# Spectra of a correlation attention by pairs of float32r products, accumulated on fixed PSUM banks

## What is computed

```python
x = x + autocorrelation(layernorm(x), ctx, ctx)        # B, L, D = 8, 512, 2048
x = x + ffn(layernorm(x))                              # w 2048x2048, bias, LoRA adapters of rank 32

corr = ifft(fft(q, axis=L) * conj(fft(k, axis=L))).real    # along L, per column
w, idx = top_k(corr, 12); w = softmax(w)
out[pos] = sum_i w_i * v[min(idx_i + pos, L - 1)]          # the index is clamped at the last row
```

## Time and profile before

| what | value |
|---|---|
| runs | 3445.2, 3446.3, 3446.85 us; median 3446.3 |
| profiled execution | 3438.6 us, its span 3436.8 us, clock 0.983 |
| PE busy | 3280.5 us (95%) |
| DVE, POOL, ACT busy | 2006.3, 1574.0, 931.3 us |
| steps 2 to 16 (from the transposes of n=1 to those of n=16) | 788.56 us, 52.57 us each |
| steps 18 to 31 (from n=17 to n=31) | 740.34 us, 52.88 us each |
| the step between them | 70.72 us |
| last step and way into the last block | 76.03 us |
| last block | 1541.7 us |

### The profile page before, as it was taken

One profiled execution on the slowest core, in us unless ns is written; L12 is line 12 of the kernel. 1 busy time (PEld: TensorE's weight loads), 2 busy tenths in 40 slices (PEclk: granted clock), 3 DMA queues, 4 the chain that ended last, 5 costly groups with the idle time before them and its releaser, 6 DMA issues. The chain is left out here.

```text
span 3436.8 us, 38078 instructions
## 1 busy us (share of the span) xinstructions
PE 3280.5 (95%) x14592; PEld 1639.7 (48%) x14592; DVE 2006.3 (58%) x2768; ACT 931.3 (27%) x1559; POOL 1574.0 (46%) x727
## 2 busy tenths in 40 slices
PE   7699999999999999999995999999999999999999
PEld 4354554554544455455542444444444444444444
DVE  4289989999888999998985232232323232232321
ACT  1434444344334444544432110111101110111100
POOL 0587888878868888887862110111001110111000
PEclk9799999999999999999998999999999999999999
DMA  7133243342342334234223611011110111011110
GB/s 310 70 113 132 98 153 110 119 153 100 129 152 108 140 127 177 103 126 147 84 101 124 228 50 59 37 38 59 50 54 29 59 49 59 37 38 59 50 50 25
DMA packets 125328, 335.59 MB, mean 98 GB/s; under 512 B 7648, under 2 KB 24160, under 8 KB 108800
## 3 DMA queue, kind: packets, MB, share of 16 engines
q1 hardware_dynamic: 125184, 333.64, 27.1%
HBM read 245.27 MB, written 88.34 MB: 97 GB/s over the span
## 5 line engine op out<-in xcount | busy, mean ns | idle before, releaser
L1248 PE MATMUL ps<-w_hi,h_hi 128*128 128x512 f16 x2048 | 780.0, 381 | 18.4 <-issue 16.9
L1250 PE MATMUL ps<-w_hi,h_lo 128*128 128x512 f16 x2048 | 779.1, 380 | 0.0
L1249 PE MATMUL ps<-w_lo,h_hi 128*128 128x512 f16 x2048 | 778.9, 380 | 0.0
L1143 POOL TENSOR_TENSOR rp<-ve,half 128x1 f32<-128x1 f32 x32 | 17.6, 549 | 1243.7 <-DVE ve L1301 1243.7
L1355 DVE SCALAR_TENSOR_TENSOR xt<-ps,w_back,xt 128x512 f32<-128x512 f32 x128 | 96.0, 750 | 757.1 <-PE ps L1250 756.1
L826 PE MATMUL ps<-op,it 128*128 128x512 f32 x1024 | 448.1, 596 | 21.0 <-DVE op L956 21.0
L752 PE MATMUL ps<-wt,fp 128*128 128x512 f16 x1536 | 339.1, 381 | 9.9 <-ACT spo L639 6.9
L1248 PEld LDWEIGHTS ps<-w_hi,h_hi 128*128 128x128 f16 x2048 | 200.9, 98 | 258.0 <-issue 27.2
L826 PEld LDWEIGHTS ps<-op,it 128*128 128x128 f32 x1024 | 195.7, 191 | 267.8 <-issue 262.3
L1250 PEld LDWEIGHTS ps<-w_hi,h_lo 128*128 128x128 f16 x2048 | 201.0, 98 | 243.9 <-issue 3.9
L1249 PEld LDWEIGHTS ps<-w_lo,h_hi 128*128 128x128 f16 x2048 | 201.0, 98 | 228.9 <-issue 3.3
(11 more groups left out here) (149 smaller groups left out, 5235.3 us busy)
## 6 DMA issues: line engine op xcount, KB each, us to landing
cg<-ctx SPq DMA_DIRECT2D x32, 1024.0 KB, 7.1
xg<-x SPq DMA_DIRECT2D x32, 1024.0 KB, 9.5
xv<-x SPq DMA_DIRECT2D x32, 1024.0 KB
x_scratch<-xv SPq DMA_DIRECT2D x32, 1024.0 KB, 7.4
xt<-x_scratch SPq DMA_DIRECT2D x32, 1024.0 KB, 5.0
out<-xt SPq DMA_DIRECT2D x32, 1024.0 KB, 4.8
xrow<-x SPq DMA_DIRECT2D x24, 1024.0 KB, 5.8
xrow<-w SPq DMA_DIRECT2D x16, 1024.0 KB, 11.3
```

What stands on the lines that cost most here:

```text
L1248: nc.tensor.matmul(ps[:, c, :], h_hi[:, k, i, :], w_hi[:, i, cols], start=(i == 0), stop=False)
L1249: nc.tensor.matmul(ps[:, c, :], h_hi[:, k, i, :], w_lo[:, i, cols], start=False, stop=False)
L1250: last = nc.tensor.matmul(ps[:, c, :], h_lo[:, k, i, :], w_hi[:, i, cols], start=False, stop=(i == KT - 1))
```

## The change

The context's spectra are made another way. GpSimd subtracts the last row from all four row tiles of ctx (`subtract_row`, in place), ScalarE rounds the result to float32r in `uh` (`high_of_u`), GpSimd leaves the rest in `cgl`, which lies on the same bytes as cg (`rest_of_u`). The tables are split likewise into fth and ftl, and fnh, fnl are the negative ones of the odd frequencies. `c_spectrum` transforms the second half of the rows, and `v_spectrum` accumulates the first half's spectrum onto the same banks, after ScalarE has copied the former out. Each of these is 4 banks x 2 row tiles x 3 products in float32r, 48 in all for a step, in place of 16 in fp32. The folds of v and z go.

Bank roles become fixed: banks 0 to 3 hold c and v spectra, the transposed weights, the first half of `weight_spectra` and `correlation`; banks 4 to 7 hold q, the second half of `weight_spectra` and `output`. `correlation(n+1)` waits for all four products of h=0. `q_spectrum` now stands behind the transposes, and nothing stands between it and `weight_spectra`. The row statistics and a sum of absolute values of w in place of its largest value go to ScalarE. The term of the last row leaves `op`: in the last block a DMA brings the last row of each batch to `vl`, and GpSimd adds it to xt, ahead of the statistics. SP's order changes: the load for q of n+3 stands first, that of ctx is for n+4 and stands later, the second piece of w is stored behind the store and load of xv, and `weights_high` of the first piece stands second in ScalarE's step.

```diff
+        cgl = nc.alloc_sbuf_tensor_at("cgl", [P, 2, TT, GC], F32R, offset=cg_at)
...
+            uh = sb("uh", [P, 4, GC], F32R, st)
...
-                    def step(b, g, more, lead, rows, convert):
+                    def step(b, g, more, lead, far, last, rows, convert):
                         n = GPB * b + g
-                        if more:
-                            sp.wait_ge(z_spec, 4 * n + 8)
-                            load_inputs(sp, *ahead(b, g, 3))
+                        if far:
+                            load_row(*ahead(b, g, 3))
+                            load_query(*ahead(b, g, 3))
...
                         sp.wait_ge(out_add, 4 * n + 4)
                         sp.dma_start(x2_g[b, :, :, g * GC:(g + 1) * GC], xv[:, :, :]).then_inc(s_st, 16)
                         if lead:
                             sp.wait_ge(s_st, 16 * n + 16)
                             load_residual(*ahead(b, g, 1))
+                        if convert:
+                            store_weights(b, g, 1)
+                            if lead:
+                                sp.wait_ge(s_wst, 32 * piece(b, g, 1) + 32)
+                                load_weights(*ahead(b, g, 1), 0)
...
+                    def forward_u(kind, k, part, fresh):
+
+                        for r in range(2):
+                            row = 2 * part + r
+                            if fresh or kind < OR:
+                                high, rest = fth[:, r, kind, :], ftl[:, r, kind, :]
+                            else:
+                                high, rest = fnh[:, r, kind - OR, :], fnl[:, r, kind - OR, :]
+                            for i, (tab, val) in enumerate(((high, uh[:, row, :]), (rest, uh[:, row, :]), (high, cgl[:, k, row, :]))):
+                                last = nc.tensor.matmul(ps[:, kind, :], tab, val, start=(fresh and r == 0 and i == 0),
+                                                        stop=(r == 1 and i == 2), skip_group_check=not fresh)
                         return last
...
                     def correlation(b, g):
                         m = GPB * b + g
                         pe.wait_ge(cp_turn, m + 1)
+                        if later(b, g):
+                            pe.wait_ge(oprod, 8 * m - 4)
+                        else:
+                            pe.wait_ge(v_out, 4)
                         for j in range(CT):
-                            if later(b, g):
-                                pe.wait_ge(oprod, 9 * m - (6 if j < 2 else 4))
...
                     def step(b, g, more, lead):
+                        transpose_w(b, g)
                         if lead:
                             q_spectrum(*ahead(b, g, 1))
-                        transpose_w(b, g)
-                        if lead:
-                            z_spectrum(*ahead(b, g, 1))
                         weight_spectra(b, g, lead)
                         if lead:
                             correlation(*ahead(b, g, 1))
                         if more:
+                            c_spectrum(*ahead(b, g, 2))
                             v_spectrum(*ahead(b, g, 2))
                         output(b, g)
...
+                        pool.wait_ge(s_xt[k], 16 * (2 * b + t // 2 + 1))
+                        pool.wait_ge(s_vl, 16 * b + 16)
+                        nc.gpsimd.tensor_tensor(xt[:, k, :], xt[:, k, :], vl[:, :], ALU.add).then_inc(vl_ok, 1)
```

More of the change, by code:

```diff
@@ L25 @@
 FP16 = mybir.dt.float16
+F32R = mybir.dt.float32r
 U32 = mybir.dt.uint32
@@ L559, in next_rows, with step @@
                         nc.gpsimd.tensor_tensor(nbn[:, :], nm1[:, :], rsn[:, :], ALU.mult).then_inc(rsn_ok, 1)
-                    def step(b, g, more, lead, rows):
+                    def step(b, g, more, lead, far, rows):
                         if more:
-                            fold_v(*ahead(b, g, 2))
                             fold_q(*ahead(b, g, 2))
-                            rest_of_q(*ahead(b, g, 2))
                         if lead:
@@ L689, in step @@
+                    def step(b, g, more, lead, far, rows, convert):
                         n = GPB * b + g
                         transposed_out(b, g)
+                        if convert:
+                            weights_high(b, g, 0)
                         if more:
                             high_of_q(*ahead(b, g, 2))
-                        if lead:
-                            store_spectrum(*ahead(b, g, 1), 1)
-                        if convert:
-                            weights_high(b, g, 0)
+                        if rows:
+                            row_statistics(b, g)
@@ L704, in step @@
                             store_spectrum(*ahead(b, g, 2), 0)
+                        if far:
+                            high_of_u(*ahead(b, g, 3))
                         if lead:
@@ L732, in _ @@
                     for g in range(GPB):
-                        step(B // 2, g, True, True, True, True)
-                    with act.Fori(B // 2 + 1, B - 1) as b:
-                        for g in range(GPB):
-                            step(b, g, True, True, True, True)
+                        step(B // 2, g, True, True, True, True, True)
                     for g in range(GPB):
-                        step(B - 1, g, g + 2 < GPB, g + 1 < GPB, g + 3 < GPB, True)
+                        step(B - 3, g, True, True, True, True, True)
@@ L740, in _ @@
+                    for g in range(GPB):
+                        step(B - 2, g, True, True, True, False, True)
+                    for g in range(GPB):
+                        step(B - 1, g, g + 2 < GPB, g + 1 < GPB, g + 3 < GPB, False, True)
                 @block.tensor
                 def _(pe):
-                    def forward(bank, kind, src):
-                        for k in range(2):
-                            last = nc.tensor.matmul(ps[:, bank, :], ft[:, k, kind, :], src[k], start=(k == 0), stop=(k == 1))
+                    def forward_u(kind, k, part, fresh):
[8 more added lines that the diff above has]
+                                                        stop=(r == 1 and i == 2), skip_group_check=not fresh)
@@ L858, in _, with corr_products @@
                 def _(dve):
-                    def corr_products_even(b, g):
+                    def corr_products(b, g):
                         m, k = GPB * b + g, g % 2
```

390 lines of the change are left out of this document (213 added, 177 removed).

## The result

The changed kernel takes 3574.99 us (median of 4 runs, 3574.11 to 3579.99) where the kernel before takes 3445.75 beside it (4 runs, 3442.3 to 3446.85): a ratio of 1.038, interval 1.0362 to 1.0398. It is 3.8% slower. Its profiled execution has a span of 3572.9 us and a mean granted clock of 0.957; before they were 3436.8 and 0.983.

What follows compares the result with a forecast made beforehand. TensorE's stream bounds the kernel before; after, the chain beside it stays uncovered. 23 (first half) + 71 (second) + 5 + 0 + 12 + 3 = +114 us on 3438.6 gives 3553, with the runs' median 8 above 3560 us; range 3480 to 3630.

Steps and rivals of the forecast that it cites:

- the chain: From q's end to the correlation: odd products, sums and out_products take 14.1 us, so TensorE stands for 3.7 us a step.
- The cover before: TensorE's own work from q's end to the correlation in the kernel before: 19.0 us, against 10.4 after.
- float32r: The 48 float32r products of the c and v spectra run at f16 pace, 0.2158 us each, 10.4 us a step.
- The clock: The correlation behind the idle gap loses 1.7 us a step, making 54.0 us; bounds 0 and 1.7.
- The second half: Products wait for the load of w's piece, there at 15.9 us: 58.0 us a step, +71 over 14 steps; bounds 54.0, 60.5.
- The ends: Outside the regular steps: start +5, changeover step 0, last step and way into the last block +12, last block +3 us.
- The step between the halves: Changeover step, 70.72 us before, made by the weight scale that both kernels have: 0 (-6 to 6) us.
- the piece comes early: Rival: w's piece arrives early and the second half runs as the first, 54.0 us a step: 3504 us, 10%.
- later: Rival: w's piece comes later (60.5 us a step), or x's load delays ScalarE's copies of the correlation: 3595 us, 10%.
- the clock holds: Rival: the clock stays up through the idle 3.7 us in both halves, -51: 3509 us, 13%.
- float32r at half the pace: Rival: the spectra's float32r products run at half the f16 pace, +311: 3871 us; 7% for all slower float32r.
- The chain was not hidden: Rival judged: the chain under 10.4 us and hidden, TensorE's stream decides, 30 steps win 3.4 us each: 3364 us, 8%.

Runs made afterwards that it cites:

- Experiment 1: Changed kernel, but the first product of h=0 waits only for the first of the two sums, the second for the other: span 3536.6 us.
- experiment 4: Changed kernel with eight, or with sixteen, more f16 products on TensorE ahead of the weights' spectra in each step: spans 3593.7 and 3585.4 us.
- experiment 2: Changed kernel, but the correlation writes banks 2 and 3 first, behind the first two products of h=0: span 3572.2 us.
- experiment 3: Changed kernel without the product of the tables' rest with u's high part, 32 float32r products for 48: span 3541.4 us.
- Experiment 5: Changed kernel, but SP stores w's second piece and loads the next first piece ahead of the store and load of xv: span 3520.8 us.
- experiment 6: Changed kernel, w's high parts and rests moved to where their engines wait: span 3522.9 us; with h=0's first product behind one sum too: 3427.75 us.
- experiment 8: Changed kernel, but GpSimd adds the last row of ctx to one column of xt only, in the last block: span 3571.4 us.
- experiment 7: Experiment 6 with the early product, plus w's first piece loaded during the first half and SP's pieces ahead of ctx's row and x: 3420.51 us.

## Why the prediction was right, and where its terms were off

The kernel took 3575 us where 3560 was forecast. **The mechanism was the one predicted**: q stands ahead of the weights' spectra, nothing covers the chain, TensorE eats what it won. 14.25 us against 14.1, idle 3.73 against 3.7, the clock lost behind it. Experiment 1 shows that this chain sets the step; experiment 4, that TensorE has room for 1.7 us of products beside it at no cost; experiments 2 and 3, that 1.6 us below it a second ring, VectorE's, is waiting, which the prediction didn't have. "It can't be shortened by starting `out_products` earlier" took the wait for both sums as given; experiment 1 needed no more than to split it. The cover before was 19.7 us in the earlier trace rows (219.44 to 239.32, less 0.17 idle), not 19.0, which changes nothing.

**float32r** was mis-sized by 5%. The 48 records run 0.227 us apart, not 0.216; with the first ones still slow it is 11.1 us in all (639.27 to 650.37), not 10.4. By forms, 400 to 1000 us, loads of float32r and f16 weights:

```profile
L832 PEld LDWEIGHTS ps<-uh,ftl 128*128 128x128 f32 x132 | 24.8, 188 | 5.1
...
L840 PEld LDWEIGHTS ps<-qh,fp 128*128 128x128 f16 x176 | 17.2, 98 | 18.3
```

The weight load takes 188 ns for 98. It is 0.7 us a step, and with 0.15 more in the chain and some 0.35 less in correlation and output it makes the 54.5 us of a step of the first half (54.45 in the mean, with n=4) against 54.0. The Trainium skill ("TensorE: Matmul & The Clock Gate", section "Weight-path perf modes") says that the fast weight load is for types other than FP32; by these rows float32r is on FP32's side (190 ns in the spectra before). Whether the load makes the pace, no run here tells.

**The clock** was the right term with too simple a rule. I charged 1.7 us for a stretch like that of the earlier trace rows; it was lost in all but one of the fifteen steps of the first half. Yet 2.0 us of idle time lost it in experiment 4, where the prediction has nothing lost behind 2.93, and 1.66 us never did.

**The second half**: 59.41 us against 58.0. 0.7 is float32r. The rest is the line on SP and the clock: ScalarE starts on the piece at 15.7 to 16.0 us in one step and at 17.5 to 19.2 in the next, not at 15.9 in all. That the shorter kind meets the 15.9 is in part luck: the store took 4.2 us for the 4.9 I had, the load 3.3 for 3.6, and what lies between them 7.2 to 7.5 for 6.3. The range of this term (54.0 to 60.5) held it. Experiment 5 shows that the order on SP cost 3.5 us a step.

**The ends.** The step between the halves was the term that failed outright: 0 with 6 us to either side, measured -9.4. I had looked only at the scale. Without it the total would have been off by 9.4 us more, so that the sum is nearer than its terms. Two rows of the kernel before, of ScalarE and TensorE in that step, show what stood there:

```profile
1026.87 1.06 ACT L619 ACTIVATE qh<-qa 128x1024 f16<-128x1024 f32 x1 [14.11 <-POOL qa L516]
```

```profile
1033.07 7.48 PE L752 MATMUL ps<-wt,fp 128*128 128x512 f16 x24 [6.92 <-ACT spo L639]
```

ScalarE waited 14.11 us for GpSimd's folds of q, ahead of which two folds of v stood that the change takes away (4.6 us, 1019.83 to 1024.47); its copies of a spectrum stood behind that wait, and TensorE was idle for 6.92 us until they were made. After, the copies stand behind the correlation, and no copy waits behind the folds. That this makes the whole 9.4 us is read from the two traces, not tried.

The start was 9.9 us later, not 6.4; runs whose edits don't touch it vary by 4 us there (228.6 to 232.7 us in experiments 5, 6 and 8). The last step and the way in took 14.2 us more, not 12: the products of `output` start 7.7 us later (38.34 behind the transposes for 30.6), and the addition is 3.6 by experiment 8. The last block took 1.8 us more where I had 3, and neither can be told from its variation.

Of the rivals, "the piece comes early" fell with the trace, "later" came half true (in every other step), "the clock holds" fell but for one step, and float32r at half the pace fell (0.227 us). The chain was not hidden, and isn't even with experiment 1, which leaves 1.66 us of it bare.

## What to carry over

When a change reorders an engine's work, count what each engine has of its own between two waits, and hold the other engines' chain against it; work taken from a stream is worth nothing where it was the cover of a chain. Look at each wait on several results for the instruction that needs only the first: here one such wait was worth 3.6 us a step, 2.1 of idle time and the clock behind it. A wait for a load belongs where its engine is idle anyway, never in front of a chain. And work put into an idle slot of VectorE isn't free while GpSimd works on the chain: 1.28 us of it cost 0.9 here.

## What the runs showed of the hardware

The clock behind idle time doesn't follow its length alone. The 32 records of the correlation behind 1.66 to 1.86 us took 7.14 to 7.17 us in every step (first halves of experiments 1, 4 with sixteen, 6 with the early product, 7); behind 1.98 to 2.12 us 8.83 to 8.86 in all steps but the first (eight more products); behind 2.24 to 2.75 us some took 7.17 and others 8.86, in experiment 7 in turn. From that kernel, two neighbouring steps of the turn:

```profile
1388.20 7.17 PE L902 MATMUL ps<-it,cp 128*128 128x256 f32 x32 [2.43 <-DVE mhi L1015]
```

```profile
1440.76 8.86 PE L902 MATMUL ps<-it,cp 128*128 128x256 f32 x32 [2.44 <-DVE mhi L1015]
```

Even 3.71 to 3.84 us left the clock alone once in each of four kernels: in the changed kernel the step of n=4 took 52.84 us, and experiments 5, 6 (slots alone) and 8 have one such step each. What decides it beside the length stays open.

VectorE and GpSimd hold each other up. The rest of w on VectorE draws a sum of GpSimd's out from 2.37 to 3.27 or 3.35 us (experiments 5 to 7). And a single VectorE addition between SBUF tiles was held for 22.83 us while GpSimd worked without a stop (experiment 1), in one step out of more than 300 profiled. The Trainium skill ("SBUF — State Buffer", section "SBUF: two separate sides") says that an instruction of GpSimd that reads SBUF and one of VectorE with two SBUF inputs take a pair of ports in turn, each for its whole length. The drawn-out sums agree with a lock, and the addition shows more than one instruction's length of waiting: some ten of GpSimd's passed ahead of this one.
